# A one-core attention and feed-forward kernel: the correlation's inverse by 16 accumulating matmuls on masked columns, the top-k search on a directly made transposed result, the output bias in the constant bin

## The reference

```
q = (layernorm(x) @ Wq + bq);  k = ctx @ Wk + bk;  v = ctx @ Wv + bv      # k, v padded to 2048 rows
c = qf.real * kf.real + 1j * -(qf.imag * kf.imag)                          # rfft along the rows
corr = irfft(c);  mean_value = mean of corr over heads and channels        # 2048 delays
weights, delay = top_k(mean_value, 15);  w = softmax(weights)
agg[l] = sum_k w[k] * v[(delay[k] + l) % 2048]
x = x + agg @ Wo + bo
x = x + ffn(layernorm(x))      # 256 -> 1024 -> 256, int8 weights, int16 activations, exact gelu
```

## Time and profile before

| | before |
|---|---|
| median of 3 runs | 202.53 us (200.09 to 204.61) |
| the profiled execution | 202.04 us |
| its span, first to last instruction | 200.2 us |
| mean granted TensorE clock | 0.939 |
| busy: PE / DVE / ACT / POOL | 86% / 77% / 54% / 16% |
| chain that ended last | PE 57%, DVE 24%, DMA 6%, ACT 5% |

### The profile page before, as it was taken

One profiled execution on the slowest core, in us unless ns is written; L12 is line 12 of the kernel. 1 busy time (PEld: TensorE's weight loads), 2 busy tenths in 40 slices (PEclk: granted clock), 3 DMA queues, 4 the chain that ended last, 5 costly groups with the idle time before them and its releaser, 6 DMA issues.

```text
span 200.2 us, 2844 instructions
## 1 busy us (share of the span) xinstructions
PE 172.7 (86%) x1051; PEld 127.5 (64%) x1054; DVE 153.5 (77%) x337; ACT 108.4 (54%) x172; POOL 31.8 (16%) x27
## 2 busy tenths in 40 slices
PE   8498999999129998989989974779999997999992
PEld 6398996447108976668985553754444455888881
DVE  0007977999998588789625799939998679999974
ACT  2225677533100264103464571789988858999930
POOL 8000000005950000000000005000592000532000
PEclk9859999999965899999999999589999999999999
DMA  3799994000000000000000000000000000001215
GB/s 109 217 290 402 411 357 158 0 5 0 0 0 0 0 3 0 2 0 0 0 3 0 0 3 0 0 0 0 5 0 0 0 0 3 0 0 56 105 52 210
DMA packets 6036, 11.96 MB, mean 60 GB/s; under 512 B 531, under 2 KB 3732, under 8 KB 5896
## 3 DMA queue, kind: packets, MB, share of 16 engines
q1 hardware_dynamic: 6024, 11.80, 17.0%
HBM read 9.70 MB, written 2.10 MB: 59 GB/s over the span
## 4 chain that ended last, share of the span: by engine, by line
PE 57%; DVE 24%; DMA 6%; ACT 5%; issue 3%; SPq 3%; DVEq 0%
PE ps L1171 12%; PE ps L1146 7%; PE ps L1141 6%; DMA arena<-wkT_dram 6%; PE ps L946 5%; DVE sm L651 4%; PE ps L965 4%; PE ps L1082 4%; DVE arena L633 3%; PE ps L997 3%; PE ps L1096 3%; PE ps L1005 2%; PE ps L1071 2%; PE ps L1121 2%; PE ps L1091 2%
## 5 line engine op out<-in xcount | busy, mean ns | idle before, releaser
L1171 PE MATMUL ps<-woutq,arena 128*128 128x256 f16 x256 | 28.7, 273 | 1.3 <-ACT arena L562 0.7
L1171 PEld LDWEIGHTS ps<-woutq,arena 128*128 128x128 f16 x256 | 24.7, 98 | 5.3 <-ACT arena L562 1.5
L547 ACT ACTIVATE arena<-ps,colv,sm 128x512 f32<-128x512 f32 x32 | 23.7, 781 | 2.1 <-PE ps L1146 0.5
L868 DVE SCALAR_TENSOR_TENSOR arena<-scr,sm,arena 128x1024 f16<-128x1024 int16 x16 | 21.3, 1372 | 0.0
L847 DVE TENSOR_REDUCE sm<-arena 128x1 f32<-128x1024 f32 (+1 forms) x17 | 18.9, 1148 | 2.5 <-ACT arena L547 2.5
L1146 PE MATMUL ps<-arena,winq 128*128 128x512 bf16 x64 | 18.6, 379 | 0.1
L1141 PE MATMUL ps<-arena,winq 128*128 128x512 bf16 x61 | 17.9, 379 | 0.7 <-ACT arena L539 0.7
L562 ACT ACTIVATE arena<-arena,sm 128x1024 f16<-128x1024 f32 x15 | 16.4, 1133 | 0.0
L946 PE MATMUL ps<-wvo,arena 128*128 128x256 f32 x64 | 15.4, 386 | 0.0
L901 PE MATMUL ps<-ones 128*128 128x256 bf16 x90 | 13.7, 311 | 1.0 <-POOL ones L349 1.0
L980 PE MATMUL ps<-arena,wqk 128*128 128x512 f32 x32 | 14.0, 594 | 0.1
(11 more groups left out here) (217 smaller groups left out, 332.3 us busy)
## 6 DMA issues: line engine op xcount, KB each, us to landing
tabs<-tab_dram SPq DMA_DIRECT2D x1, 2424.0 KB, 15.7
arena<-x_dram SPq DMA_DIRECT2D x4, 512.0 KB, 12.5
out_dram<-arena SPq DMA_DIRECT2D x8, 256.0 KB, 2.1
arena<-ctx_in_dram SPq DMA_DIRECT2D x3, 400.0 KB
arena<-winT_dram SPq DMA_DIRECT2D x1, 1024.0 KB, 17.0
arena<-wout_dram SPq DMA_DIRECT2D x1, 1024.0 KB, 19.2
arena<-ctx_in_dram SPq DMA_DIRECT2D x2, 200.0 KB
arena<-wqT_dram SPq DMA_DIRECT2D x1, 256.0 KB, 9.7
```

The source lines that it names most:

```text
L547: a.activation(H[:, f, 512 * c:512 * c + 512], bank("M1", n), ACT.Gelu, bias=colv[:, 6 + f:7 + f], scale=sc1[:, f:f + 1]).then_inc(S["h_re ...
L868: v.scalar_tensor_tensor(out=part, in0=scr16[:, n % 4, :], scalar=rf[:, f:f + 1], in1=piece(Hhi, n), op0=ALU.mult, op1=ALU.subtract).then_ ...
L1171: return t.matmul(o[k // 2][:, 256 * (k % 2):256 * (k % 2) + 256], part[:, t0:t0 + 128], woutq[:, f, :], start=start, stop=stop)
```

## The change

Four edits.

1. **The inverse (IN).** DVE no longer multiplies the table `P`. It writes `ab` masked by `J` into a cleared tile `abx` (128 x 16 groups of 65 columns, the group's four bins at stride 16), 64 numbers in each partition. PE multiplies each group's 64 columns of `abx` with that group's 32 columns of `P`, 16 products that accumulate in one bank, 64 x 32. What was masked and added on DVE is now a copy of 64 x 32. POOL clears `abx` once, ahead of its wait for QP.
2. **The search.** The last inverse step is made transposed at once (TM, 16 x 128, two products, weights `ins`). DVE searches it directly. ACT copies it to `tms` after the row search, PE transposes it back into ME behind BC, and DVE copies that into `mean` after the 15 largest are known.
3. **The attention's output bias.** POOL's addition to x is gone. The bias is added to the constant bin of the result's spectrum instead: 16 columns of `cx` for each half, one instruction on ACT behind the copy of OO 0 and one on DVE behind that of OO 1. The bias comes as two more columns of `colv`; `rowv` and its transfer halve.
4. **Order.** In `order` ME moves from ahead of TM to behind BC.

```
@@ @@ order
-        order += [("VP", 0), ("IN", 0), ("VP", 1), ("ME", 0), ("TM", 0), ("VP", 2), ("BC", 0)]
+        order += [("VP", 0), ("IN", 0), ("VP", 1), ("TM", 0), ("VP", 2), ("BC", 0), ("ME", 0)]
@@ @@ POOL
+            g.memset(abx[:], 0.0).then_inc(S["abx_zero"], 1)
             filled(pool, "QP", 7)
             g.memset(BUT, 0.0).then_inc(S["bt_zero"], 1)
             pool.wait_ge(S["bt_zero"], 1)
-            pool.wait_ge(S["ld_row"], 16)
-            pool.wait_ge(S["xh_a"], 2)
-            pool.wait_ge(S["xh_d"], 2)
             x3 = xs.rearrange("p (b d) -> p b d", b=NB)
-            g.tensor_tensor(x3, x3, rowv[:, 0:D].unsqueeze(1).to_broadcast([128, NB, D]), ALU.add).then_inc(S["xb_ready"], 1)
-            pool.wait_ge(S["xb_ready"], 1)
@@ @@ ACT
+            act.wait_ge(S["cand_ready"], 1)
+            a.copy(tms[:], bank("TM", 0)[0:NB, 0:128]).then_inc(S["tm_ready"], 1)
+            act.wait_ge(S["mean_ready"], 1)
             act.wait_ge(S["v16_ready"], 1)
...
+                if i == 0:
+                    ins_.then_inc(S["z_a"], 1)
+                    act.wait_ge(S["z_a"], 1)
+                    ins_ = a.activation(constant_bin(0), constant_bin(0), ACT.Identity, bias=colv[:, 14:15])
+                ins_.then_inc(S["os_a"], 1)
@@ @@ DVE
-            v.tensor_tensor(pr2, tb3("P"), ab.unsqueeze(2).to_broadcast([128, NG, 32]), ALU.mult)\
-             .then_inc(S["ab_ready"], 1)
+            dve.wait_ge(S["abx_zero"], 1)
+            v.tensor_tensor(abx.rearrange("p (g c) -> p g c", g=NG)[:, :, 0:NS:NG], ab.unsqueeze(2).to_broadcast([128, NG, NJ]),
+                            tb("J")[:, 0:NS:NG].unsqueeze(1).to_broadcast([128, NG, NJ]), ALU.mult).then_inc(S["ab_ready"], 1)
...
-            link(v.tensor_tensor(own.rearrange("s (g c) -> s g c", g=NG), bank("IN", 0)[0:NS, :].rearrange("s (g c) -> s g c", g=NG),
-                                 tb("G", NS).unsqueeze(2).to_broadcast([NS, NG, NM]), ALU.mult))
-            v.tensor_reduce(ins[:], own.rearrange("s (g c) -> s c g", g=NG), AX.X, ALU.add).then_inc(S["own_ready"], 1)
+            v.tensor_copy(ins[:], bank("IN", 0)[0:NS, 0:NM]).then_inc(S["ins_ready"], 1)
             vproj(1)
-            filled(dve, "ME", 0)
-            v.tensor_copy(mean, bank("ME", 0)[:, 0:NB]).then_inc(S["mean_ready"], 1)
...
             dve.wait_ge(S["v16_ready"], 1)
+            filled(dve, "ME", 0)
+            v.tensor_copy(mean, bank("ME", 0)[:, 0:NB]).then_inc(S["mean_ready"], 1)
+            dve.wait_ge(S["mean_ready"], 1)
...
+                if i == 1:
+                    ins_.then_inc(S["z_d"], 1)
+                    dve.wait_ge(S["z_d"], 1)
+                    ins_ = v.tensor_scalar(constant_bin(1), constant_bin(1), colv[:, 15:16], None, ALU.add)
+                ins_.then_inc(S["os_d"], 1)
-            dve.wait_ge(S["xb_ready"], 1)
@@ @@ PE
             o = take_bank(pe, "IN", 0)
-            done(t.matmul(o[0:NS, :], tb("J"), pr2.rearrange("p g c -> p (g c)"), start=True, stop=True))
+            for g in range(NG):
+                last = t.matmul(o[0:NS, 0:NM], abx[:, NS * g:NS * g + NS], tb3("P")[:, g, :], start=(g == 0), stop=(g == NG - 1))
+            done(last)
             vproj(1)
-            pe.wait_ge(S["own_ready"], 1)
-            o = take_bank(pe, "ME", 0)
+            pe.wait_ge(S["ins_ready"], 1)
+            o = take_bank(pe, "TM", 0)
             for r in range(2):
-                last = t.matmul(o[:, 0:NB], tb("FR", NS)[:, 128 * r:128 * r + 128], ins[:, r:NM:2],
+                last = t.matmul(o[0:NB, 0:128], ins[:, r:NM:2], tb("FR", NS)[:, 128 * r:128 * r + 128],
                                 start=(r == 0), stop=(r == 1))
             done(last)
-            pe.wait_ge(S["mean_ready"], 1)
-            o = take_bank(pe, "TM", 0)
-            done(t.transpose(o[0:NB, 0:128], mean, tb("I")))
             vproj(2)
...
             done(t.matmul(o[:, 0:256], ones[0:NB, :], cand, start=True, stop=True))
+            pe.wait_ge(S["tm_ready"], 1)
+            o = take_bank(pe, "ME", 0)
+            done(t.transpose(o[:, 0:NB], tms[:], tb("I", NB)[:, 0:NB]))
             vproj(3)
```

More of the change, by code:

```diff
@@ L147, in build @@
         woutq = sb("woutq", [128, 8, D], f16)
-        colv = sb("colv", [128, 14])
-        rowv = sb("rowv", [128, 2 * D])
+        colv = sb("colv", [128, 16])
+        rowv = sb("rowv", [128, D])
         scr = sb("scr", [128, 4, 1024])
@@ L160, in build @@
         ins = sb("ins", [NS, NM])
+        tms = sb("tms", [NB, 128])
+        abx = sb("abx", [128, NG * 65])
         sm = sb("sm", [128, 704])
@@ L197, in build @@
         names = ("ld_F ld_wqk ld_tab ld_wv ld_win ld_wout ld_col ld_row "
[L198 to L199 removed]
+                 "pe dve_link act_link pool_const bu_ready z_a z_d bt_zero x2b_ready nz_ready "
+                 "xh_a xh_d qt_ready wqk_ready qc_ready bkb_ready qb_ready ownq_ready qbs_ready wvo_ready bvo_ready bvb_ready gram_a gram_d abx_zero tm_ready ab_ready ins_ready "
                  "mean_ready cand_ready v16_ready ex_ready eq_ready wn_ready "
@@ L244, in build @@
             "VP": lambda i: [(S["vh_ready"], i + 1)],
-            "IN": lambda i: [(S["own_ready"], 1)],
+            "IN": lambda i: [(S["ins_ready"], 1)],
             "ME": lambda i: [(S["mean_ready"], 1)],
@@ L250, in build @@
             "WB": lambda i: [(S["winq_ready"], i + 1)],
-            "TM": lambda i: [(S["cand_ready"], 1)],
+            "TM": lambda i: [(S["tm_ready"], 1)],
             "BC": lambda i: [(S["v16_ready"], 1)],
@@ L317, in _ @@
             sp.dma_start(tabs[:, at["UT"][0]:NCONST], tab[:, at["UT"][0]:NCONST]).then_inc(S["ld_tab"], 16)
-            sp.dma_start(rowv[:], rows[0:1, :].to_broadcast([128, 2 * D])).then_inc(S["ld_row"], 16)
+            sp.dma_start(rowv[:], rows[0:1, :].to_broadcast([128, D])).then_inc(S["ld_row"], 16)
             sp.dma_start(wraw[:, 0:2048].rearrange("p (f d) -> p f d", f=8),
@@ L383, in _ @@
             pool.wait_ge(S["rs2_ready"], 1)
+            pool.wait_ge(S["ld_row"], 16)
             pool.wait_ge(S["yq_ready"], 4)
-            g.tensor_tensor(x3, x3, rowv[:, D:2 * D].unsqueeze(1).to_broadcast([128, NB, D]), ALU.add).then_inc(S["x2b_ready"], 1)
+            g.tensor_tensor(x3, x3, rowv[:].unsqueeze(1).to_broadcast([128, NB, D]), ALU.add).then_inc(S["x2b_ready"], 1)
             pool.wait_ge(S["hsc_ready"], 1)
@@ L393, in spectrum, with constant_bin @@
             return cx[:, h * 2048:(h + 1) * 2048].rearrange("p (b s r) -> p b s r", b=NB, r=2)[:, :, 16 * q:16 * q + 16]
+        def constant_bin(h):
+            return cx[:, h * 2048:(h + 1) * 2048:128]
         def spread(buf, h, bq):
@@ L498, in _ @@
                 filled(act, "OO", i)
-                a.copy(spectrum(0, i // 2), bank("OO", i).rearrange("p (s b r) -> p b s r", b=NB, r=2)).then_inc(S["os_a"], 1)
+                ins_ = a.copy(spectrum(0, i // 2), bank("OO", i).rearrange("p (s b r) -> p b s r", b=NB, r=2))
+                if i == 0:
[3 more added lines that the diff above has]
+                ins_.then_inc(S["os_a"], 1)
             a.activation(warm[:, 0:1], one, ACT.Sqrt)
@@ L755, in _ @@
                 filled(dve, "OO", i)
-                v.tensor_copy(spectrum(1, i // 2), bank("OO", i).rearrange("p (s b r) -> p b s r", b=NB, r=2)).then_inc(S["os_d"], 1)
-            dve.wait_ge(S["xb_ready"], 1)
+                ins_ = v.tensor_copy(spectrum(1, i // 2), bank("OO", i).rearrange("p (s b r) -> p b s r", b=NB, r=2))
+                if i == 1:
[3 more added lines that the diff above has]
+                ins_.then_inc(S["os_d"], 1)
             y3 = yn.rearrange("p (b d) -> p b d", b=NB)
@@ L1219 @@
         "wo": L0_xattn_Wo, "winT": np.asarray(L0_ffn_W_in).T, "wout": L0_ffn_W_out,
-        "cols": np.concatenate([cols(L0_xattn_bk), cols(L0_xattn_bq), cols(L0_xattn_bv), cols(L0_ffn_b_in)], 1),
-        "rows": np.concatenate([np.asarray(L0_xattn_bo), np.asarray(L0_ffn_b_out)])[None],
+        "cols": np.concatenate([cols(L0_xattn_bk), cols(L0_xattn_bq), cols(L0_xattn_bv), cols(L0_ffn_b_in), cols(L0_xattn_bo)], 1),
+        "rows": np.asarray(L0_ffn_b_out)[None],
         "tab": tab,
```

## The result

The changed kernel took 193.5 us (median of 4, 193.14 to 193.97) beside 203.42 us before (median of 4, 200.09 to 204.61). The ratio was 0.961, 95% interval 0.951 to 0.972; it compares undisturbed executions only (of the kernel before those at 200.09 and 202.53, mean 201.3 us), which is why it isn't the ratio of the two medians. Two later sets on two other chips gave 191.94 us and 0.954 (0.946 to 0.961), and 192.5 us and 0.950 (0.943 to 0.956). The kernel is faster, by 4 to 5%. The forecast was 192.0 us, which is 5.2% against the 202.53 us it started from and 4.6% against the 201.3 us of the ratio; the first measurement gave 3.9%. By the time, the kernel came out 1.5 us above the forecast.

What follows compares the result with a forecast made beforehand. PE was taken to bound the kernel, waiting 8.0 us at QB2 for DVE, stalled behind POOL's addition. 202.04 - 10.84 + 0.7 = 191.9 us profiled, 192.0 as median; own range 190.8 to 193.0, with rivals 189.0 to 195.5.

Steps and rivals of the forecast that it cites:

- Step 1: Ahead of QB2: without POOL's addition, L651 takes about 0.2 us, PE has no wait and QB2 starts 8.04 us earlier.
- Step 2: QB2 to IN: PE at the higher clock, waiting about 0.9 us before the last UU part; IN starts 10.84 us earlier.
- the clock falls all the same: Rival, 52 to 63 us: PE's clock drops anyway, only the stall is won, 194.7 us; chance 0.12.
- Step 3: At IN: the 16 products, 32 instructions, take 2.2 us, 1.1 us extra on PE.
- Step 4: From IN to the search and L713: hidden DVE work wins nothing; everything behind L713 and EQ comes 0.7 us later.
- Step 5: Clearing of abx, constant-bin additions and shorter bias transfer cost nothing; the clearing would cost 0.9 us if it stopped DVE uncovered.
- The sum: Whole kernel: 202.04 - 10.84 + 0.7 = 191.9 us for the profiled execution; median forecast 192.0.
- one of the rivals: The later low clock at 125 to 130 us shrinks; at full clock 1.9 us less, 190.1 us; chance 0.10.
- the forecast's own range: Whole kernel: 190.8 to 193.0 us, from the products (2.0 to 3.3) and half a microsecond of run-to-run spread.

Runs made afterwards that it cites:

- e1: Kernel before with only the output bias moved into the constant bin and POOL's addition to x removed; 191.85 us, ratio 0.951.
- e3: Kernel before with POOL's addition to x cut into 16 instructions of 256 columns at the same place; 199.02 us, ratio 0.988.
- e8: Changed kernel with POOL's clearing of BUT (128 x 2048) made to run beside DVE's quantising of wout; 195.33 us.
- e9: Changed kernel with the old inverse: one product over 512 columns, mask and sum on DVE, no abx; 192.37 us, ratio 0.946.

## Why the prediction was right or wrong

**Step 1, the stall: right.** L651 was to take 0.2 us and took 0.17; QB2 was to start 8.04 earlier and started 8.17 earlier, without a wait. That it is POOL's instruction which stops DVE's was read from a match of 0.03 us; e1, e3 and e8 show it.

**Step 2, what is late next: the order right, the clock wrong.** PE was to wait 0.9 us for DVE's last GR copy and waited 0.99. But "PE does not idle, so I take the higher clock" was the step that failed: it priced the last UU part, WB and VP 0 at the higher level, and 3.4 us of them ran at the lower. I had looked for a low clock where PE's long idle stretch had been and had counted the new short wait only as time. IN was to start 10.84 us earlier and started at 64.67 instead of 73.82, 9.15 earlier. The difference, 1.7, is the low stretch: 0.4 in UU, 0.8 in WB, 0.4 in VP 0. I had a rival for it ("the clock falls all the same") at 0.12 and 2.8 us; it came in all three profiles of the changed kernel, at 1.7 us. A weight near one half, as the seven profiles with the wait have it, and that price would have put the forecast some 0.8 us higher. Why the clock falls behind so short a wait in some profiles and not in others stays open.

**Step 3, the 16 products: right.** 2.2 us was the value taken, 2.05 was measured:

```profile
64.67 2.05 PE L1048 MATMUL ps<-tabs,abx 128*64 128x32 f32 x32
...
66.76 0.18 DVE L701 COPY ins<-ps 64x32 f32<-64x32 f32 x1 [1.02 <-PE ps L1048]
...
69.48 0.28 DVE L706 MAX8 sm<-ps 16x8 f32<-16x128 f32 x1
...
73.60 0.24 DVE L723 TENSOR_SCALAR sm<-sm 128x16 f32<-128x16 f32 x1
```

The masked write (0.27) won nothing, as said; VP 0 hid it.

The estimate of 2.6 us by the sustained spacing in the Trainium skill ("TensorE: Matmul & The Clock Gate", section "Back-to-back issue gap") does not agree with the trace, where 32 instructions in 2.05 us are 64 ns each; its 81 ns are for 128 moving columns, and these products have 32.

**Step 4, the search: the sum right to 0.1, its inner term not.** Counted from IN's start, the search and L713 were to come 0.7 later each. The search is at 69.48 - 64.67 = 4.81 against 78.19 - 73.82 = 4.37, 0.44 later, and L713 (now L723) 8.93 against 8.34, 0.59 later. The search itself was sized 0.3 too late. That DVE's mask and sum were free is shown by e9: having them back costs nothing.

**Step 5: right.** The additions in the constant bin (0.33 and 0.24) end before the next OO bank is full, EQ to TR is 22.0 in both, and the clearing of `abx` was hidden, as it fell where DVE ran nothing of the kind that e8 shows stopped. The Trainium skill ("SBUF — State Buffer", section "Who interferes with whom") says that a DVE instruction in a two-port mode and a GpSimd instruction contend and that the one issued first blocks the other fully, without an exception for a clearing. e8 agrees as to the blocking, 2.04 us instead of 0.35; which of the two was issued first its profile doesn't settle.

**The sum.** -10.84 + 0.7 was forecast for the profiled execution, and -8.9 was measured. Stage by stage it is -9.15 up to IN, +0.6 from IN to EQ, -0.6 from TR to M1, and +0.1 behind that: 9.1 us less span, and 8.9 less of device time. The -0.6 is one of the rivals, in part: the later low stretch (rows at 125 to 130 in the earlier trace rows) lasted 3.4 us instead of 6.8. Two errors of opposite sign, 1.7 and 0.6, and that 0.2 leave the profiled execution 1.2 us above the 191.9 of the sum. That it was not more is luck. In the two later sets the changed kernel took 191.94 and 192.5 us, inside the forecast's own range, although both profiled executions have the low stretch that the working had left out: a time that fits does not bear out step 2.

## What to carry to other kernels

Where a tiny DVE operation shows microseconds, look at what POOL is doing, clearings included, and move or remove POOL's instruction; cutting it in 16 pieces left a ratio of 0.988 where removing it gave 0.951. An edit that turns a long PE wait into a short one should still be priced with a fall of the clock behind it. Replacing DVE work that was hidden behind a PE stage by more PE instructions is a loss even where the DVE work that goes (the mask and the sum, 1.7 us here) is longer than the PE work that comes (1.0).

## What the runs showed of the hardware beyond that

A wait of PE of only 1.0 us, in a stretch otherwise filled with small f32 products, was followed within 0.5 to 1.9 us by 3.4 us at 1.2 GHz in four of seven profiles that had it (in one of the four, e8, two shorter waits stood just ahead), and in none of the three that had not. The counts are too small to show that the wait is the cause. Single executions of one program on one core also differ by up to 4 us ahead of the first product that needs all of x (45.8 to 49.6), so that profiles of two kernels have to be compared stage by stage.
